# Reordering the loads, the spreading product and GpSimd's work ahead of the main products of a conditioned LoRA kernel

## What is computed

```python
x = x + einsum('bct,bcd->bdt', x, W0[cond])          # W0: 16 x 32 x 32
base  = einsum('bsi,oi->bso', x, W)                  # W: 512 x 512
low   = einsum('bsi,bir->bsr', x, lora_A[label])     # lora_A: 5 x 512 x 32, label in 0..2
delta = einsum('bsr,or->bso', low, lora_B_w) * 0.5   # lora_B_w: 512 x 32
x = x + base + delta
```

## Time and profile before

| | us |
|---|---|
| median of 3 runs | 87.47 (87.38 to 87.57) |
| the profiled execution, own time | 88.03 |
| its span, first to last instruction | 86.2 |
| TensorE busy | 81.8 (95%) |
| VectorE busy | 55.0 (64%) |
| ScalarE busy | 39.7 (46%) |
| GpSimd busy | 23.1 (27%) |

### The profile page before, as it was taken

The page is one execution under the profiler, slowest core; times in us unless marked ns, Lnnn a source line. Parts: engine busy times, 40 slices in busy tenths (PEclk is TensorE's granted clock), DMA queues, the critical chain, the costliest instruction groups (busy, mean ns, idle before and its releaser), DMA issues.

```text
span 86.2 us, 1395 instructions
## 1 busy us (share of the span) xinstructions
PE 81.8 (95%) x455; PEld 71.5 (83%) x455; DVE 55.0 (64%) x116; ACT 39.7 (46%) x80; POOL 23.1 (27%) x38
## 2 busy tenths in 40 slices
PE   5998999999999999999999999999999999999950
PEld 4697999998888988898889888988898888889940
DVE  3736586979971795479545974499349933731550
ACT  0552663417545464347345716561754273405430
POOL 5402786872467003700260007000700000000000
PEclk9999999999999999999999999999999999999999
DMA  1799998091000593792048303750240014000606
GB/s 33 168 278 379 193 206 148 20 229 25 0 8 15 199 245 54 234 237 39 0 179 230 97 0 108 250 143 0 105 153 0 0 64 180 0 8 7 237 17 226
DMA packets 12393, 10.16 MB, mean 118 GB/s; under 512 B 1508, under 2 KB 9572, under 8 KB 12388
## 3 DMA queue, kind: packets, MB, share of 16 engines
q1 hardware_dynamic: 11728, 9.77, 41.2%
q0 software_dynamic: 512, 0.26, 1.7%
q10 hardware_dynamic: 148, 0.07, 0.3%
HBM read 5.90 MB, written 4.19 MB: 117 GB/s over the span
## 4 chain that ended last, share of the span: by engine, by line
PE 87%; DMA 6%; SPq 2%; DVE 1%; issue 0%
PE p_u L588 15%; PE p_u L589 15%; PE p_u L590 15%; DMA w_sb<-in_L_cond_W 6%; PE p_low L578 4%; PE p_low L574 4%; PE p_low L573 4%; PE p_u L599 4%; PE p_y L606 4%; PE p_y L605 4%; PE p_y L608 4%; PE p_y L590 2%; PE p_y L589 2%; PE p_y L588 2%; PE p_u L616 2%; PE p_u L622 1%
## 5 line engine op out<-in xcount | busy, mean ns | idle before, releaser
L254 POOL DMA_INDIRECT w_sel<-in_L_cond_weights,w_row x16 | 15.8, 990 | 32.0 <-DVE diag L500 29.1
L589 PE MATMUL p_u<-m_lo,xt_hi 128*128 128x512 f32 (+1 forms) x60 | 22.6, 377 | 0.0
L588 PE MATMUL p_u<-m_hi,xt_hi 128*128 128x512 f32 (+1 forms) x60 | 22.6, 377 | 0.0
L590 PE MATMUL p_u<-m_hi,xt_lo 128*128 128x512 f32 (+1 forms) x60 | 22.5, 375 | 0.0
L397 DVE STREAM_TRANSPOSE xt<-x_sb 128x512 f32<-128x512 f32 x14 | 15.3, 1096 | 0.7 <-DMA x_sb<-in_x 0.7
L417 DVE TENSOR_TENSOR u_lo<-p_u,u_hi 128x512 fp32r<-128x512 f32 (+1 forms) x15 | 9.3, 651 | 9.9 <-ACT u_hi L314 9.9
L411 DVE TENSOR_TENSOR xt_lo<-xt,xt_hi 128x512 fp32r<-128x512 f32 x14 | 9.5, 681 | 7.5 <-ACT xt_hi L309 7.4
L319 ACT ACTIVATE y_sb<-p_y 128x512 f32 (+1 forms) x13 | 7.7, 591 | 12.2 <-PE p_y L608 12.2
L590 PEld LDWEIGHTS p_u<-m_hi,xt_lo 128*128 128x128 f32 x60 | 11.3, 188 | 2.1
L588 PEld LDWEIGHTS p_u<-m_hi,xt_hi 128*128 128x128 f32 x60 | 11.3, 188 | 1.9
L589 PEld LDWEIGHTS p_u<-m_lo,xt_hi 128*128 128x128 f32 x60 | 11.3, 188 | 1.8
(11 more groups left out here) (92 smaller groups left out, 124.9 us busy)
## 6 DMA issues: line engine op xcount, KB each, us to landing
x_sb<-in_x SPq DMA_DIRECT2D x28, 128.0 KB, 3.6
out<-y_sb SPq DMA_DIRECT2D x7, 512.0 KB, 3.1
w_sb<-in_L_cond_W SPq DMA_DIRECT2D x4, 256.0 KB, 5.1
x_rows<-in_x SPq DMA_DIRECT2D x2, 256.0 KB, 4.8
out<-y_sb SPq DMA_DIRECT2D x2, 256.0 KB, 2.1
a_sb<-in_L_cond_lora_A SPq DMA_DIRECT2D x1, 256.0 KB, 7.0
w_sel<-in_L_cond_weights,w_row POOLq DMA_INDIRECT x16, 2.8
a_sb<-in_L_cond_lora_A ACTq DMA_DIRECT2D x1, 64.0 KB, 2.0
```

Of the source, the lines that this page charges most:

```text
L254: nc.gpsimd.indirect_dma_start(out=w0_sel[:, t, :], out_offset=None, in_=W0_rows, in_offset=bass.IndirectOffsetOnAxis(ap=w0_row[:, t:t + 1 ...
L588: mm(to, xt_hi[:, slot, c, rows], m_hi[:, c, cols], start=(c == 0 and half != 1), stop=False)
L589: mm(to, xt_hi[:, slot, c, rows], m_lo[:, c, cols], start=False, stop=False)
L590: mm(to, xt_lo[:, slot, c, rows], m_hi[:, c, cols], start=False, stop=False)
```

## The change

cond and label are issued first on ScalarE's queue, A0 third, and behind it the W blocks 1 and 0, which leave SyncE's queue. One warming product goes; the spreading product stands in its place, ahead of the adapters' transposes. VectorE copies the spread ids before W1's addition. GpSimd converts the ids ahead of the four selections of `fold_id`, computes the row numbers before the additions to W's blocks 3 and 2, issues the first gather behind those, then the mask and `a_diff`, the second gather, and `ad_lo`.

```diff
--- before.py
+++ after.py
@@ -200,7 +200,7 @@
 
             sp.dma_start(bw_sb[:], Bw.rearrange("(o p) r -> p o r", p=P)).then_inc(s_bw_in, 16)
             sp.dma_start(x_rows[:, 0], x_tile[0]).then_inc(s_rows_in[0], 16)
-            for o in W_ORDER:
+            for o in W_ORDER[2:]:
                 sp.dma_start(w_sb[:, o], W[P * o:P * (o + 1), :]).then_inc(s_w_in[o], 16)
             sp.dma_start(x_rows[:, 1], x_tile[1]).then_inc(s_rows_in[1], 16)
             sp.dma_start(a_sb[:, 1:NL].rearrange("p l c r -> p l (c r)"), A_cols[:, 1:NL]).then_inc(s_a_in, 16)
@@ -235,20 +235,14 @@
                                     pattern=[[-1, P]], channel_multiplier=1).then_inc(s_pool, 1)
             pool.wait_ge(s_pool, 3)
             nc.gpsimd.memset(fold_id[:], 0.0).then_inc(s_pool, 1)
+            pool.wait_ge(s_cond_in, 16)
+            pool.wait_ge(s_label_in, 16)
+            nc.gpsimd.tensor_copy(ids_r[:], ids_i[:]).then_inc(s_ids, 1)
             for j in range(Q):
                 pool.wait_ge(s_pool, 4 + j)
                 nc.gpsimd.affine_select(out=fold_id[:], in_=fold_id[:], compare_op=ALU.not_equal, fill=1.0,
                                         base=-R * j, pattern=[[-1, R]], channel_multiplier=1).then_inc(s_pool, 1)
 
-            pool.wait_ge(s_cond_in, 16)
-            pool.wait_ge(s_label_in, 16)
-            nc.gpsimd.tensor_copy(ids_r[:], ids_i[:]).then_inc(s_ids, 1)
-
-            for o in W_ORDER[2:]:
-                pool.wait_ge(s_w_in[o], 16)
-                w_diag = w_sb[:, o, P * o:P * (o + 1)]
-                nc.gpsimd.tensor_tensor(w_diag, w_diag, ident[:], ALU.add).then_inc(s_diag_right, 1)
-
             def gather(t):
 
                 nc.gpsimd.indirect_dma_start(
@@ -256,12 +250,10 @@
                     in_offset=bass.IndirectOffsetOnAxis(ap=w0_row[:, t:t + 1], axis=0),
                 ).then_inc(s_w0_in[t // 2 % 2], 16)
 
-
             pool.wait_ge(s_group, BT)
             pool.wait_ge(s_row_of, 1)
             pool.wait_ge(s_ids_sb, 1)
             cond_v = ids_all[:, 0].rearrange("p (k b) -> p b k", b=BT)
-            pool.wait_ge(s_diag_right, 2)
             for j in range(BT):
                 quad = slice(R * j, R * (j + 1))
                 if j:
@@ -269,6 +261,12 @@
                 nc.gpsimd.tensor_scalar(w0_row[quad], cond_v[quad, j], float(S), row_of[quad, 0:1],
                                         ALU.mult, ALU.add).then_inc(s_w0_row, 1)
             pool.wait_ge(s_w0_row, BT)
+            for o in W_ORDER[2:]:
+                pool.wait_ge(s_w_in[o], 16)
+                w_diag = w_sb[:, o, P * o:P * (o + 1)]
+                nc.gpsimd.tensor_tensor(w_diag, w_diag, ident[:], ALU.add).then_inc(s_diag_right, 1)
+            gather(0)
+            pool.wait_ge(s_diag_right, 2)
             nc.gpsimd.tensor_scalar(keep[:], ids_all[:, 1], -1.0, group[:, 0:1], ALU.add,
                                     ALU.is_equal).then_inc(s_keep, 1)
 
@@ -278,12 +276,10 @@
             nc.gpsimd.tensor_tensor(a_diff[:], a_sb[:, 1:NL].rearrange("p l c r -> p c l r"),
                                     a_sb[:, 0].unsqueeze(2).broadcast_to([P, C, Q, R]),
                                     ALU.subtract).then_inc(s_adiff, 1)
+            gather(1)
             pool.wait_ge(s_adiff, 1)
             pool.wait_ge(s_adhi, 1)
             nc.gpsimd.tensor_tensor(ad_lo[:], a_diff[:], ad_hi[:].bitcast(F32), ALU.subtract).then_inc(s_adlo, 1)
-            pool.wait_ge(s_w0_row, BT)
-            gather(0)
-            gather(1)
 
             for p in range(1, PAIRS):
                 if p >= 2:
@@ -293,9 +289,11 @@
 
         @blk.scalar
         def _(act):
-            act.dma_start(a_sb[:, 0].rearrange("p c r -> p (c r)"), A_cols[:, 0]).then_inc(s_a0_in, 16)
             act.dma_start(ids_i[:, 0], cond.unsqueeze(0)).then_inc(s_cond_in, 16)
             act.dma_start(ids_i[:, 1], label.unsqueeze(0)).then_inc(s_label_in, 16)
+            act.dma_start(a_sb[:, 0].rearrange("p c r -> p (c r)"), A_cols[:, 0]).then_inc(s_a0_in, 16)
+            for o in W_ORDER[:2]:
+                act.dma_start(w_sb[:, o], W[P * o:P * (o + 1), :]).then_inc(s_w_in[o], 16)
 
             def split_rows(u, bank):
 
@@ -465,6 +463,8 @@
                 w_diag = w_sb[:, o, P * o:P * (o + 1)]
                 nc.vector.tensor_tensor(w_diag, w_diag, ident[:], ALU.add).then_inc(s_diag, 1)
 
+            dve.wait_ge(s_ids_all, 1)
+            nc.vector.tensor_copy(ids_all[:].rearrange("p u b -> p (u b)"), p_fold[:, 0:2 * B]).then_inc(s_ids_sb, 1)
             dve.wait_ge(s_pool, 3)
             diag_w(0)
             dve.wait_ge(s_pool, 4 + Q)
@@ -474,8 +474,6 @@
             dve.wait_ge(s_group, 2 * BT + 4)
             nc.vector.tensor_copy(fold_to[:], fold_parts[:]).then_inc(s_group, 1)
             diag_w(1)
-            dve.wait_ge(s_ids_all, 1)
-            nc.vector.tensor_copy(ids_all[:].rearrange("p u b -> p (u b)"), p_fold[:, 0:2 * B]).then_inc(s_ids_sb, 1)
             split_rows(0, p_low)
 
             def split_m(half, b):
@@ -635,7 +633,7 @@
 
 
             pe.wait_ge(s_warm, 1)
-            for i in range(WARM):
+            for i in range(WARM - 1):
                 mm(p_low[:], warm[:], warm[:].unsqueeze(1).broadcast_to([P, 4, P]), start=True, stop=True)
 
             def transpose_groups(bank, source):
@@ -650,13 +648,13 @@
                 mm(p_fold[:, 0:2 * B], ones_r[:], ids_r[:].rearrange("p u b -> p (u b)"), start=True,
                    stop=True).then_inc(s_ids_all, 1)
 
+            spread_ids()
             pe.wait_ge(s_pool, 3)
             pe.wait_ge(s_rep, 2)
             transpose_groups(p_y[0], bw_rep).then_inc(s_bT, 1)
             pe.wait_ge(s_rep, 4)
             transpose_groups(p_y[1], a_rep).then_inc(s_aT, 1)
             transpose_rows(0, p_low)
-            spread_ids()
             pe.wait_ge(s_diag, 1)
             transpose_w(0)
             pe.wait_ge(s_diag, 2)
```

## The result

| | before | changed |
|---|---|---|
| median of all 6 runs, us | 87.42 | 89.45 |
| the same without those the ratio leaves out, us | 87.42 | 89.07 |
| the profiled execution, own time | 88.03 | 88.86 |
| its span | 86.2 | 87.0 |
| main products start, in that trace | 10.73 | 11.52 |

The ratio is 1.0199 (95% interval 1.0158 to 1.0241): slower by 2.0%, some 1.75 us. The forecast was 88.2, that is +0.7, with a range of 87.0 to 89.0, so the sign was right and the size was not.

What follows compares the result with a forecast made beforehand. TensorE's main products run dense for 72.5 us, so their start at 10.73 decides, bound by W0, W2 and x_rows 1 landings. W0 0.7 later makes 88.03 into 88.73; the median, 0.56 lower, gives 88.2, range 87.0 to 89.0 us.

Steps and rivals of the forecast that it cites:

- I take +0.7: W0's transposes on TensorE: chosen delay of 0.7 us from W0 landing later, out of 0.1 to 1.5.
- The slow level: TensorE's early transposes: 0.21 us spacing lasting longer after a break, giving 88.0 to 89.0 us; rival, chance 0.08.
- The term that decides, W1 and W0 on ScalarE's queue: Start-up loads: two queues take equal turns from 3.4 us, so W0 lands later and its transposes move 0.1 to 1.5 us.
- At today's rates: W0's load: 1048 to 1178 KB after 3.4 us finish at 7.29 to 7.64, landing at 8.4 to 8.8 us.
- The upper end of +1.2 to +1.5: W0's load: the delay if splitting queues gives no bandwidth and turns run at the earlier trace's rates.
- The sum: Whole kernel: nothing shrinks behind W0's transposes, so 88.03 becomes 88.73 profiled; median 0.56 lower, forecast 88.2 us.
- Spreading product: TensorE's start: product starts near 3.75, costs 0.25, adapter transposes near 4.0; net +0.1 there, -0.15 at W1's transposes.
- A0: Third on ScalarE's queue: lands at 3.6 to 4.2, costing its transposes 0 to 0.3 us, covered by the W0 wait.
- The break at 3.35: TensorE after five warming products: a break of about 0.4 us, which might delay the faster level by 2 us.
- GpSimd and VectorE's new wait: Reordered GpSimd work, and VectorE waiting for the spreading product before W1's addition: no cost; ad_lo starts about 13.9 us.
- The rivals of cancelling and gaining: Whole kernel: cancelling gives 87.4 to 87.6 us, chance 0.16; faster order gives 87.0 to 87.2, chance 0.24.

Runs made afterwards that it cites:

- experiment 2: The kernel before with one edit, W1 and W0 issued on ScalarE's queue behind A0, cond and label; ratio to before 1.0175.
- after_again: The changed kernel run once more with no edit; ratio to before 1.0201, its traced execution 89.31 us.
- after_six_warm: The changed kernel with the sixth warming product put back, W1 and W0 still on ScalarE's queue; ratio to before 1.0162.
- w_on_sp_again: Second trace of the changed kernel with W1 and W0 back on SyncE's queue and five warming products; 89.12 us.
- experiments 3 and 6: The changed kernel with W1 and W0 back on SyncE's queue, 1.0074 of before; then that kernel with the sixth warming product put back, 0.9987.
- experiment 4: The kernel before with cond and label issued ahead of A0 and nothing else; ratio to before 0.9990.
- experiment 6: Two edits, each alone, to the changed kernel with all W on SyncE's queue: sixth warming product back, 0.9987 of before; GpSimd's old order, 1.0078.
- experiment 8: The changed kernel with six warming products instead of five, W1 and W0 still on ScalarE's queue; ratio to before 1.0162, its trace 89.43 us.

## Why the prediction was wrong

The step that failed is the size of one term, "I take +0.7" for W1 and W0 on ScalarE's queue; alone this edit costs 1.5 us (experiment 2). It was mis-sized because W0's later landing was set against 7.25, while the kernel before had W0 at 5.9 and 6.2 in its two other traces. The slow level, left out of the sum, is a second and smaller omission.

- **The term that decides, W1 and W0 on ScalarE's queue: mechanism right, its baseline wrong.** "At today's rates" was one execution's rate. The landing forecast for the changed kernel, 7.3 to 8.8, held (7.97, 8.24, and 7.98 and 7.74 in the two other kernels with this split). The turns are seen in the packets, 282 against 258. The start of the count was wrong: the blocks' packets begin at 4.57, not at 3.4. From there two blocks and as much beside them, 1048 KB, take until 7.34 at the 378 GB/s of 4.5 to 7.1 us, and W0 landed 0.63 after that. The late start and a rate above the 217 of the earlier trace rows largely offset each other, which was luck. The Trainium skill (DMA: Bandwidth & Descriptors, "Queues, rings and completion order") has each engine take turns between queues; from 4.5 us on these traces agree. By its section "Issuing engines are not separate DMA queues" issuing from several engines saves only issue time; from 3.4 to 7.1 us the four traces with W1 and W0 on ScalarE's queue moved 343 to 374 GB/s and the twelve with all of W on SyncE's 262 to 370, so no gain stands out here either. The upper end of +1.2 to +1.5 that this rule gave in the prediction is near the measured loss for another reason: it meant a landing at 8.4 to 8.8, which did not come. What was mis-sized was what the landing is compared with: W0 at 5.9 to 6.2 in the other two traces of before instead of 7.25, where it isn't a bound at all. The move is 1.8 to 2.1 us for W0; with TensorE's own order of 9.96 as the floor it is 1.4 to 1.6 at the main products, and 1.5 by experiment 2.
- **The sum.** It carried the 0.56 us between profiled execution and median unchanged to both sides, as if it lay outside the chain. It lay in W0's and x_rows 1's landings, which is where the change acted; in the changed kernel no trace has W0 early. Trace against trace, +0.7 forecast and +0.8 found, is luck: it sets a long execution of before against the fastest of the changed kernel.
- **The slow level** was priced as a rival by itself, at 0.08. It is an addition: of the nine traces of kernels with the spreading product first, four (`after_again`, `after_six_warm`, `w_on_sp_again`, and that of GpSimd's old order) keep 0.21 us spacing to 8.4 us or later; of the ten with it in its old place, those of before among them, none does beyond 7.2. That is a count over single traces and not an experiment on the product's place. The missing sixth product is worth 0.7% with W on SyncE's queue (experiments 3 and 6), how much of it by this level stays open; beside a late W0 most of it is hidden, 1.020 against 1.0175, with intervals that overlap.
- **Spreading product**: it started at 3.48 and the adapters' transposes at 3.88, against 3.75 and 4.0 forecast; the ids were converted earlier than said, but the product took 0.40 and not 0.25, a price read from the earlier trace rows where TensorE was at its fast level. **A0**: landed at 4.46 where 4.2 was the latest I gave, and its transposes wait until 5.33, 0.45 later than TensorE could, against 0 to 0.3; hidden in time, as said (experiment 4). The break at 3.35 that the prediction put beside it was never there.
- **GpSimd and VectorE's new wait**: nothing in the time, as forecast (experiment 6; ad_lo started at 13.48), though GpSimd's additions now fell beside VectorE's addition to W0 and that one took 0.19 longer in the first trace. x_rows 1 landed at 8.3 and not 9.5; it was also issued 0.96 earlier, and two of the three traces of before have it at 9.5 and one at 8.4, so what moved it is not shown.
- **The rivals of cancelling and gaining** needed a W0 as early as in the earlier trace rows; it was never before 7.7.

The Trainium skill (TensorE: Matmul & The Clock Gate, "Part 1: The HAM clock gate") says that the moment of the rise differs from run to run of one kernel, by about half a microsecond either way. The traces agree that it differs but by far more, with 5.5 us and later than 9.1 for the changed kernel.

**Open**: what makes transfers late in one execution and not in the next; why ScalarE's blocks begin to move only 2.6 us after their issue; what keeps the slow level, since six products came with a fast level in the traces with all of W on SyncE's queue and not in `after_six_warm`, and no rest explains it by itself (0.73 us in experiment 4 left it fast, a shorter one in experiment 8 slow); and the mechanism of the 0.5% with five products.

## What to carry to other kernels

A transfer that others wait for should have few bytes ahead of it counting both queues: of two blocks moved to a second queue, which had to share with what stood on the first, the second came 2 us later, while one block moved alone cost nothing. Ask of a profiled execution whether its slack is a typical one: when it lies above the median, as here, the difference can sit in the very wait that the change moves, and the change must then be costed from the median's side; a second trace of the unaltered kernel would have shown it. Warming products that look like filling may be worth something: here one fewer cost 0.5% to 0.7%, so removing one is to be measured by itself.

## What was not expected of the hardware

The same kernel moved its first blocks at 217 GB/s in one execution and 314 in another, and W0 landed 1.4 us apart. TensorE's slow spacing of 0.21 us lasted to between 4.2 and 10.4 us from the same start at 1.05, at a granted clock of 1.00 throughout, so that column does not show this level. An addition of 128x128 on VectorE took 0.48 us beside one on GpSimd and 0.29 without.
